# Mixing and conv products with loads of 64 rows and 128 columns in place of four quadrants

## Time and profile before

| | |
|---|---|
| median of 3 runs | 2088.99 us (2088.69 to 2089.23) |
| the profiled execution | 2088.94 us |
| its span, first to last instruction | 2087.1 us |
| PE busy, matmuls | 2078.6 us, 22231 records |
| PE busy, weight loads | 1980.7 us, 22231 records |
| DVE, POOL, ACT busy | 1526.5, 963.6, 309.7 us |

### The profile page before, as it was taken

One profiled execution on the slowest core, in us unless ns is written; L12 is line 12 of the kernel. 1 busy time (PEld: TensorE's weight loads), 2 busy tenths in 40 slices (PEclk: granted clock), 3 DMA queues, 4 the chain that ended last, 5 costly groups with the idle time before them and its releaser, 6 DMA issues.

```text
span 2087.1 us, 61023 instructions
## 1 busy us (share of the span) xinstructions
PE 2078.6 (100%) x22231; PEld 1980.7 (95%) x22231; DVE 1526.5 (73%) x5265; ACT 309.7 (15%) x924; POOL 963.6 (46%) x1318
## 2 busy tenths in 40 slices
PE   9999999999999999999999999999999999999999
PEld 8999999999999999999999999999999999999998
DVE  6766766666667666666787778877777788887776
ACT  4111111111111111111211111111111111111110
POOL 4644444444444444444854444544444445454442
PEclk9999999999999999999999999999999999999999
DMA  6534334334343343344433333333333433333332
GB/s 240 141 96 113 107 97 113 104 108 112 94 112 108 94 117 103 106 114 118 127 96 104 107 100 97 94 94 94 94 103 106 101 99 94 94 94 94 94 107 80
DMA packets 152180, 222.76 MB, mean 107 GB/s; under 512 B 18256, under 2 KB 100176, under 8 KB 152144
## 3 DMA queue, kind: packets, MB, share of 16 engines
q1 hardware_dynamic: 151808, 221.97, 38.9%
q10 hardware_dynamic: 336, 0.30, 0.1%
HBM read 121.47 MB, written 100.73 MB: 106 GB/s over the span
## 4 chain that ended last, share of the span: by engine, by line
PE 99%; DVE 0%; DMA 0%; ACT 0%; issue 0%; DVEq 0%; ACTq 0%
PE psB L1061 79%; PE psB L1087 8%; PE psT L1039 7%; PE psT L1002 3%; PE psB L1158 1%; DMA outb<-in_condw 0%; PE psT L1017 0%; PE psT L1095 0%; PE psB L1095 0%; DVE Ylo L736 0%; DVE Wlo L744 0%; DVE outb L779 0%; ACT Whi L557 0%; DVE outb L772 0%; PE psB L1074 0%
## 5 line engine op out<-in xcount | busy, mean ns | idle before, releaser
L1061 PE MATMUL psB<-Whi,Yhi 128*128 128x384 f32 x3024 | 723.3, 346 | 1.7 <-DVE outb L779 1.6
L1061 PE MATMUL psB<-Wlo,Yhi 128*128 128x384 f32 x3024 | 703.3, 340 | 0.0
L1061 PE MATMUL psB<-Whi,Ylo 128*128 128x384 f32 x3024 | 701.2, 339 | 0.0
L1061 PEld LDWEIGHTS psB<-Whi,Yhi 128*128 128x128 f32 x3024 | 537.9, 189 | 26.6 <-issue 2.3
L1061 PEld LDWEIGHTS psB<-Whi,Ylo 128*128 128x128 f32 x3024 | 549.9, 189 | 0.0
L1061 PEld LDWEIGHTS psB<-Wlo,Yhi 128*128 128x128 f32 x3024 | 548.6, 188 | 0.1
L441 POOL TENSOR_TENSOR res<-res,bias 128x256 f32<-128x256 f32 x256 | 180.1, 735 | 545.5 <-DMA res<-x_scratch 545.5
L891 DVE STREAM_TRANSPOSE HT<-hw 32x32 f32<-32x32 f32 x1968 | 398.1, 202 | 25.1
L470 POOL TENSOR_TENSOR Ylo<-Y,Yhi 128x256 fp32r<-128x256 f32 x244 | 190.8, 802 | 319.4 <-ACT Yhi L545 319.4
L779 DVE TENSOR_TENSOR outb<-psB,res 128x384 f32<-128x384 f32 x381 | 223.1, 672 | 126.0 <-PE psB L1087 126.0
L431 POOL TENSOR_TENSOR res<-Xraw,bias 128x256 f32<-128x256 f32 x248 | 218.4, 914 | 207.2 <-DVE outb L779 197.8
(11 more groups left out here) (129 smaller groups left out, 1577.3 us busy)
## 6 DMA issues: line engine op xcount, KB each, us to landing
x_scratch<-outb SPq DMA_DIRECT2D x64, 512.0 KB, 2.7
x_block_scratch<-outb SPq DMA_DIRECT2D x512, 64.0 KB, 1.9
Xraw<-x_block_scratch SPq DMA_DIRECT2D x128, 256.0 KB, 5.2
res<-x_scratch SPq DMA_DIRECT2D x64, 512.0 KB, 4.7
out<-outb SPq DMA_DIRECT2D x64, 512.0 KB, 2.9
Xraw<-in_x SPq DMA_DIRECT2D x62, 512.0 KB, 3.4
row<-row_scratch SPq DMA_DIRECT2D x126, 64.0 KB, 4.1
stage<-in_l0w SPq DMA_DIRECT2D x8, 580.5 KB, 12.4
```

Source lines behind the costliest of these rows:

```text
L1061: last = mm(psB[:, 3 * par + b, 0:cols], y, w[:, k, BANK0[b]:BANK0[b] + cols], start=(k == 0 and y is yh and w is Whi), stop=(k == KT - 1 ...
```

## The change

`mix_squares` becomes `mix_halves`, and `convolve` is edited in the same way. The loop over `m` goes: one matmul takes all 128 positions of a slice as stationary columns, with the 64 rows of one sample, and writes all 128 output partitions of bank `a`. Outputs, operands and semaphores are the same as before.

```diff
--- before.py
+++ after.py
@@ -993,15 +993,13 @@
                 if not (isinstance(n, int) and n == 0):
                     pe.wait_ge(y_chunk, NC * n)
 
-            def mix_squares(j, par):
+            def mix_halves(j, par):
 
                 half = slice(0, C), slice(C, P)
                 for k in range(KT):
-                    for m in range(2):
-                        for a in range(2):
-                            last = mm(psT[half[m], a, k * C:(k + 1) * C],
-                                      x_tile(j, par)[half[a], k * P + m * C:k * P + (m + 1) * C],
-                                      M[half[a], half[a]], start=True, stop=True)
+                    for a in range(2):
+                        last = mm(psT[:, a, k * C:(k + 1) * C], x_tile(j, par)[half[a], k * P:(k + 1) * P],
+                                  M[half[a], half[a]], start=True, stop=True)
                 last.then_inc(mixed, NC)
 
             def mix(j, par, c):
@@ -1033,11 +1031,10 @@
                 half = slice(0, C), slice(C, P)
                 for k in range(2):
                     for w in range(PRODUCTS):
-                        for m in range(2):
-                            for a in range(2):
-                                to = (k * PRODUCTS + w) * C
-                                last = mm(psT[half[m], a, to:to + C], Xs[half[a], w, 2 * i + k, half[m]],
-                                          CT[half[a], k, w, :], start=True, stop=True)
+                        for a in range(2):
+                            to = (k * PRODUCTS + w) * C
+                            last = mm(psT[:, a, to:to + C], Xs[half[a], w, 2 * i + k, :],
+                                      CT[half[a], k, w, :], start=True, stop=True)
                 last.then_inc(mixed, 2)
 
             def base(j, par, layer, k, banks=range(3), y_chunks=None):
@@ -1219,7 +1216,7 @@
                     if k == TURN_AFTER[lay] and pe_turns(*before(j, par), lay0) is not None:
                         turn(*before(j, par))
                     if lay1 == 0 and k == MIX_AFTER:
-                        mix_squares(*after(j, par))
+                        mix_halves(*after(j, par))
                     if lay1 == 1 and k in conv_after:
                         convolve(conv_after.index(k))
                     if k == UP_AFTER[lay] and lay0 is not None:
```

## The result

| | before | after |
|---|---|---|
| median | 2089.11 us (2088.69 to 2089.46, 4 runs) | 2247.46 us (2245.93 to 2250.79, 4 runs) |
| profiled execution's span | 2087.1 us | 2243.9 us |
| ratio to before | | 1.0757, 95% interval 1.0745 to 1.077 |

The change makes the kernel 158 us slower. The forecast was 2248.0 us with a range of 2230 to 2264.

The account below looks back on a forecast made before the run. PE (TensorE) was taken as the bound, busy 2078.6 of 2087.1 us. 189 blocks x 0.843 us = +159.3 us, 52 in mixing and 108 in conv, led from a median of 2088.99 to 2248 us, range 2230 to 2264.

Parts of the forecast that it names:

- PE is the bound, one for one: Whole kernel: PE busy 2078.6 of 2087.1 us and 99% of the chain, so any change in its need is paid in full.
- The round goes by the width of the load: Mixing and conv blocks: loads 128 columns wide instead of 64 lengthen a round from 0.0577 to 0.111 us, +0.807 us a block.
- rival C: Block loads limited by elements, or fast weight load returning: round stays at 0.058 us, no change, 2089 us; chance 0.04.
- The row halves load together: Mixing and conv blocks: the two 64x128 loads of a round run beside each other; taken as so, no row showing it.
- rival D: Row halves in a block do not load together: round 0.223 us, +2.58 us a block, +488 us, 2577 us; chance 0.03.
- Entering and leaving unchanged: Transitions around each block: no change taken, with bounds of -0.26 us a block (the gap vanishes) and +0.05 us.
- rival F: Main forecast with a cheaper entry to each block: -0.26 us x 189 = -49 us, 2199 us; chance 0.04.
- Half the instructions save nothing: Each block: 16 matmuls removed save only stagger inside a round, -0.013 us a block; instructions in the round's shadow cost nothing.
- Rival E: Instruction count sets a block's round, 0.0072 us each: four fewer give -0.43 us a block, -81 us, 2008 us; chance 0.03.
- The block and the sum: Mixing and conv blocks: 0.807 + 0.049 - 0.013 = +0.843 us each, 189 blocks, +159.3 us.
- DVE and POOL keep their busy times: Page after the change: DVE and POOL keep their busy times and lose share, with no wait added.
- The clock: Granted clock stays at 1.00; falling below full in the blocks was named as a way to be wrong, without a size.

## Why the prediction was right

- **PE is the bound, one for one.** Right: 189 blocks longer by 0.84 us gave 158.4 us of median. No other wait appeared on the path; the page after has the same 1.6 us at the layer boundary. That the median lies within 1 us of the forecast is in part luck, since the four runs spread over 4.9 us.
- **The round goes by the width of the load.** Right, and the step on which all hung: 0.111 us forecast, 0.111 in the trace. The start-up's matmuls had shown it before (8 and 64 moving columns at one price, 16, 64 and 128 loaded columns at three), and the runs with 32 moving columns confirmed it in the blocks themselves. One of these rows was weaker than the prediction took it: L1095 moves 128 columns too, and at 0.056 us for each 64 its stream alone takes the 0.111 us, so it could neither price the 128-wide load nor speak against a fast load (rival C). Of the 128-wide loads only L1169's pair, 0.106 us, did; the block of the kernel after, with 64 moving columns and 0.111, settles both.
- **The row halves load together.** Assumed then, with no row for it. The block of 1.93 us itself is against 3.7 (rival D), and the run with one half alone shows that the second costs nothing. It holds because the loop alternates them.
- **Entering and leaving unchanged.** Right: 15.6 and 32.1 us of gap as before. What the tiled form costs in all, 0.33 us a block, had not been seen in full: I had read only the 0.26 ahead of it, and priced rival F by that.
- **Half the instructions save nothing.** Right in size: 0.013 us of stagger a block. Rival E's price of 0.0072 us an instruction was wrong; about 0.004 us is what the run with eight tiles has (0.0084 a pair, pauses aside).
- **The block and the sum.** +0.843 us forecast, 1.93 - 1.09 = +0.84 measured. The forecast span would be 2087.1 + 159.3 = 2246.4, measured 2243.9; the 2.5 us between are the 2.3 us that the base groups lost.
- **DVE and POOL keep their busy times.** Only nearly: DVE went from 1526.5 to 1511.3 us, POOL from 963.6 to 961.0. DVE's part is one line, L736 (Ylo), with 134 instructions in 107.7 us before and in 90.8 after; why these became faster is open. On no path, so without effect.
- **The clock.** It stayed at 1.00 in the profiled execution. That it could have fallen was named, beside a wait on DVE, as what would make the forecast wrong from another side, and the run with the halves in turn shows that the danger was real for blocks of 3.3 us, behind them and not in them. With blocks of 1.93 us it is small but there: the slowest of the four runs, 2250.79 us, has a mean of 0.997, and (1 - 0.997) x 2249 = 7 us is the most that this costs, enough for its 4.8 us over the profiled one. The run of 2248.94 us has a mean of 1.0, and its 3 us are open. With the conv alone changed, the two slower runs of four have 0.998.

## What to carry to other kernels

Where a matmul's moving side is short, count columns of the stationary side: in these blocks an f32 pass cost the larger of 0.058 us for 64 loaded columns (0.111 for 128) and 0.056 for 64 moving ones, with 64 rows or 128. The base products, in float32r, are another case: 8.18 / 45 = 0.182 us for about 384 moving columns. Splitting the array by columns halves the time of a round, and giving the split up to halve the instruction count nearly doubles it; four load and matmul pairs a round cost nothing here, eight did. Put the tiles that are to run together next to each other in program order. Each tiled block cost 0.33 us of going in and out, which speaks for few and long blocks, though no run gathered them, and the blocks of 3.3 us with one half at work brought the clock down.

## What the runs showed of the hardware that was not expected

- A tiled block costs 0.33 us of transition, of which 0.13 us lies in the base work behind it, where no idle time is shown.
- TensorE ran loads of different row halves beside each other over about four loads of distance, and no further.
- Behind some blocks of 3.3 us with one row half at work at a time, the granted clock fell to 0.50, which cost some 68 us in all. With one row half left out altogether (blocks of 1.93 us) its mean was 0.999 or 1.0. What in the longer blocks brings it down was not tried.
- With eight tiles a round, the first 32 loads of a block go out in 0.19 us, and behind them a load with its matmul each 0.0084 us, with a pause each 32 loads; the pauses cost more than the pace.
